# Negated row maxima of an attention kernel: one identity product and a DMA in place of eight transposes and two row copies

## What is computed

```python
scores = jnp.einsum('bhqd,bhkd->bhqk', q, k) * scale
scores = jnp.where(ki > qi, -jnp.inf, scores)
attn = jax.nn.softmax(scores.astype(jnp.float32), axis=-1).astype(q.dtype)
out = jnp.einsum('bhqk,bhkd->bhqd', attn, v)
```

## Time and profile before

| | us |
|---|---|
| median of 3 runs | 1096.61 |
| lowest and highest | 1094.93, 1104.24 |
| the profiled execution | 1103.35 |
| its span in the profile | 1101.6 |

### The profile page before, as it was taken

One profiled execution on the slowest core, in us unless ns is written; L12 is line 12 of the kernel. 1 busy time (PEld: TensorE's weight loads), 2 busy tenths in 40 slices (PEclk: granted clock), 3 DMA queues, 4 the chain that ended last, 5 costly groups with the idle time before them and its releaser, 6 DMA issues.

```text
span 1101.6 us, 16371 instructions
## 1 busy us (share of the span) xinstructions
PE 1026.8 (93%) x5792; PEld 795.2 (72%) x5792; DVE 661.8 (60%) x1195; ACT 420.3 (38%) x669; POOL 635.3 (58%) x363
## 2 busy tenths in 40 slices
PE   3889999997999999986979999999999999999996
PEld 2666777774877777653768888878888788887885
DVE  6666887885787887852755445624446344553454
ACT  3215665563136565543132222333224222242222
POOL 4105878899227788887445445465544654546452
PEclk9989999998999999977979999999999999999998
DMA  6322332333212233211232232433233423233331
GB/s 217 96 51 77 84 85 69 91 90 97 93 48 75 75 81 84 73 39 58 97 133 86 91 109 87 134 114 115 86 115 105 143 86 114 87 115 134 114 105 39
DMA packets 52509, 104.38 MB, mean 95 GB/s; under 512 B 10848, under 2 KB 10848, under 8 KB 52192
## 3 DMA queue, kind: packets, MB, share of 16 engines
q1 hardware_dynamic: 52448, 103.59, 30.4%
HBM read 70.00 MB, written 8.39 MB: 71 GB/s over the span
## 4 chain that ended last, share of the span: by engine, by line
PE 76%; POOL 8%; DVE 7%; issue 5%; ACT 2%; SPq 1%; DMA 1%; POOLq 0%; ACTq 0%; DVEq 0%
PE ps L1159 18%; PE ps L1160 18%; PE ps L1161 18%; PE ps L1243 7%; PE ps L1215 6%; PE ps L1277 5%; POOL gu_lo L616 2%; POOL p_sum L600 2%; PE ps L1291 1%; PE ps L1226 1%; POOL acc L662 1%; PE ps L1251 1%; DMA x_in<-x 1%; DVE xt_lo L927 1%; POOL dn_lo L622 1%
## 5 line engine op out<-in xcount | busy, mean ns | idle before, releaser
L616 POOL TENSOR_TENSOR gu_lo<-gu_raw,gu_hi 128x1024 fp32r<-128x1024 f32 x64 | 155.2, 2425 | 234.4 <-ACT gu_hi L821 234.4
L950 DVE CUSTOM_DVE_ANT_0 ps<-ps,mask_q 128x384 f32<-128x384 f32 (+7 forms) x256 | 190.2, 778 | 38.1 <-PE ps L1215 35.2
L1159 PE MATMUL ps<-xt_hi,gu_hi 128*128 128x512 f32 x512 | 202.2, 395 | 7.6 <-POOL gu_lo L616 7.6
L1025 DVE TENSOR_TENSOR h<-ps,silu 128x512 f32<-128x512 f32 x64 | 44.2, 690 | 266.7 <-PE ps L1161 239.5
L1160 PE MATMUL ps<-xt_lo,gu_hi 128*128 128x512 f32 x512 | 201.3, 393 | 0.0
L1161 PE MATMUL ps<-xt_hi,gu_lo 128*128 128x512 f32 x512 | 201.0, 393 | 0.0
L1031 DVE TENSOR_TENSOR h_lo<-h,h_hi 128x512 fp32r<-128x512 f32 x64 | 154.2, 2409 | 2.2
L821 ACT ACTIVATE gu_hi<-gu_raw 128x1024 fp32r<-128x1024 f32 x64 | 67.9, 1061 | 147.7 <-PE ps L1161 110.1
L1243 PE MATMUL ps<-q_stack,k_stack 98*128 98x512 f32 (+3 forms) x384 | 116.0, 385 | 4.1 <-DVE q_stack L969 1.6
L1159 PEld LDWEIGHTS ps<-xt_hi,gu_hi 128*128 128x128 f32 x512 | 97.5, 190 | 29.4 <-issue 8.9
L1215 PE MATMUL ps<-k_stack,q_stack 96*128 96x512 f32 (+3 forms) x384 | 111.4, 366 | 5.2 <-DVE m_full L950 2.7
(11 more groups left out here) (124 smaller groups left out, 1817.7 us busy)
## 6 DMA issues: line engine op xcount, KB each, us to landing
gu_raw<-gu_w SPq DMA_DIRECT2D x64, 512.0 KB, 3.8
dn_raw<-dn_w SPq DMA_DIRECT2D x64, 256.0 KB, 2.6
x_in<-x SPq DMA_DIRECT2D x32, 256.0 KB, 4.1
q_stack<-st_hi SPq DMA_DIRECT2D x128, 64.0 KB, 2.0
k_stack<-st_hi SPq DMA_DIRECT2D x128, 64.0 KB, 2.0
qk_raw<-qk_w SPq DMA_DIRECT2D x16, 256.0 KB, 3.0
q_stack<-st_lo SPq DMA_DIRECT2D x64, 64.0 KB, 2.0
k_stack<-st_lo SPq DMA_DIRECT2D x64, 64.0 KB, 2.0
```

The lines of the kernel that those rows point to most:

```text
L616: nc.gpsimd.tensor_tensor(gu_lo[:, s], gu_raw[:, s], gu_hi[:, s].bitcast(F32), ALU.subtract).then_inc(gu_split, 1)
L950: nc.vector.tensor_tensor_reduce(out=scores, in0=scores, in1=mask_q[:, SEQ - (t + 1) * P:], scale=1.0, scalar=MASKED, op0=ALU.add, op1=ALU ...
L1159: nc.tensor.matmul(dst, hi, r_hi, start=start, stop=False)
```

## The change

The maxima now go to rows by one product and one DMA. DVE writes the 32 columns (hi for head 0 and 1, eight tiles each, then the rests in the same order) into a small tile `m_cols`. The PE multiplies `m_cols`, as the stationary operand, by an identity of type float32r: the result has 32 partitions, one for each (part, head, tile), and 128 columns, one for each query of the tile. DVE copies these 32x128 values to `m_rows` (a corner of `x_in[:, 4]`), and ACT's queue issues one DMA that lays them out as two rows of 2048 in `q_stack`. `scores(g, 0)` waits for the DMA (`m_loaded`). DVE frees the two ring banks once its copy is done. On the PE the product stands behind three slices of the projection and ahead of the late values. Slice 3 now stands ahead of the scores of round 0. POOL makes `ident_r` once at the start.

```diff
-        m_spread = x_in[:, 4, 0:TT * M_STEP].rearrange("p (t n) -> p t n", n=M_STEP)
+        m_rows = x_in[0:2 * 2 * TT, 4, P:2 * P]
...
+            nc.gpsimd.tensor_copy(ident_r[:, :], ident[:, :]).then_inc(pool_hi, 1)
...
@@ scalar
-            def max_rows(g):
-
-                use = use_of_rows(g)
-                act.wait_ge(bank_full, use + NCH)
-                first = use % RING * CH
-                nc.scalar.activation(q_stack[QK_ROWS:ROWS, g % 2, 0], ps_cols[0:2, first:first + SEQ], ACT.Copy).then_inc(m_rows0, 1)
+            def load_maxima(g):
+
+                act.wait_ge(m_copied, g + 1)
+                to = q_stack[QK_ROWS:ROWS, g % 2].rearrange("p h (t n) -> p (h t) n", n=P)
+                act.dma_start(to.bitcast(F32), m_rows).then_inc(m_loaded, DMA)
 
             def body(g):
                 projected = g + 2 < ALL_UNITS
+                load_maxima(g)
                 if g % UNITS:
                     copy_acc(g - 1)
-                max_rows(g)
@@ vector
-                negative = ps[:, use % RING, 0:2 * TT].rearrange("p (t h) -> p t h", h=2)
-                m_hi, m_lo = m_spread[:, :, 0:HD + 1:HD].bitcast(F32R), m_spread[:, :, 1:HD + 2:HD].bitcast(F32R)
+                negative = ps[:, use % RING, 0:2 * TT].rearrange("p (h t) -> p h t", h=2)
+                m_hi, m_lo = (m_cols[:, n * 2 * TT:(n + 1) * 2 * TT].rearrange("p (h t) -> p h t", h=2) for n in range(2))
...
             def max_rows(g):
 
                 use = use_of_rows(g)
                 vec.wait_ge(bank_full, use + NCH)
-                first = use % RING * CH
-                nc.vector.tensor_copy(q_stack[QK_ROWS:ROWS, g % 2, 1], ps_cols[HD:HD + 2, first:first + SEQ]).then_inc(bank_free, NCH)
+                if g:
+                    vec.wait_ge(m_loaded, DMA * g)
+                nc.vector.tensor_copy(m_rows, ps[0:2 * 2 * TT, use % RING, 0:P]).then_inc(m_copied, 1)
+                vec.wait_ge(m_copied, g + 1)
+                vec.sem_inc(bank_free, NCH)
@@ tensor
-                for t in range(TT):
-                    at_col = use % RING * CH + t * P
-                    last = nc.tensor.transpose(ps_cols[:, at_col:at_col + P], x_in[:, 4, t * M_STEP:t * M_STEP + P], ident[:, :])
-                last.then_inc(bank_full, NCH)
+                nc.tensor.matmul(ps[0:2 * 2 * TT, use % RING, 0:P], m_cols[:, :], ident_r[:, :], start=True, stop=True).then_inc(bank_full, NCH)
...
                 if r == 0:
-                    pe.wait_ge(m_rows0, g + 1)
-                    pe.wait_ge(bank_free, use_of_rows(g) + NCH)
+                    pe.wait_ge(m_loaded, DMA * (g + 1))
...
-                project_next(0, 0)
+                project_next(0, 0, 1, 2)
+                transpose_maxima(g)
                 if has_sums(g):
                     values(g - 1, LATE_VALUES)
-                transpose_maxima(g)
-                project_next(0, 1)
                 maxima_of_next(0)
-                project_next(0, 2)
-                maxima_of_next(1)
-                pe.wait_ge(m_rows0, g + 1)
-                maxima_of_next(2)
+                project_next(0, 3)
+                maxima_of_next(1, 2)
                 scores(g, 0)
-                maxima_of_next(3)
-                project_next(0, 3)
-                maxima_of_next(4, 5)
+                maxima_of_next(3, 4, 5)
                 scores(g, 1)
```

More of the change, by code:

```diff
@@ L88 @@
 assert sorted(m[:2] for m in MAXES) == [(h, t) for h in range(2) for t in range(TT)]
-M_STEP = 48
 MAX_OFF = [sum(m[2] for m in MAXES[:n]) for n in range(len(MAXES))]
@@ L274, in build @@
             ident = sb(att, "ident", [P, P])
+            ident_r = sb(att, "ident_r", [P, P], F32R)
+            m_cols = sb(att, "m_cols", [P, 2 * 2 * TT], F32R)
             ident_bf = sb(att, "ident_bf", [P, P], BF16)
@@ L337, in build @@
         m_ready = sem("m_ready")
-        m_rows0 = sem("m_rows0")
+        m_copied = sem("m_copied")
+        m_loaded = sem("m_loaded")
         score_full = sem("score_full")
@@ L561, in _ @@
             pool.wait_ge(pool_hi, 8)
+            nc.gpsimd.tensor_copy(ident_r[:, :], ident[:, :]).then_inc(pool_hi, 1)
+            pool.wait_ge(pool_hi, 9)
             nc.gpsimd.tensor_copy(ident_bf[:, :], ident[:, :]).then_inc(consts_made, 1)
@@ L565, in _ @@
             pool.wait_ge(consts_made, 2)
-            made = [8]
+            made = [9]
             def split(hi, lo, raw, done):
@@ L956, in negated @@
                 vec.wait_ge(bank_free, use)
-                negative = ps[:, use % RING, 0:2 * TT].rearrange("p (t h) -> p t h", h=2)
-                m_hi, m_lo = m_spread[:, :, 0:HD + 1:HD].bitcast(F32R), m_spread[:, :, 1:HD + 2:HD].bitcast(F32R)
-                nc.vector.tensor_scalar(negative.bitcast(F32R), m_full[:, :, :], -1.0, None, ALU.mult).then_inc(dve_unit, 1)
+                negative = ps[:, use % RING, 0:2 * TT].rearrange("p (h t) -> p h t", h=2)
+                m_hi, m_lo = (m_cols[:, n * 2 * TT:(n + 1) * 2 * TT].rearrange("p (h t) -> p h t", h=2) for n in range(2))
+                m = m_full.rearrange("p t h -> p h t")
+                nc.vector.tensor_scalar(negative.bitcast(F32R), m, -1.0, None, ALU.mult).then_inc(dve_unit, 1)
                 vec.wait_ge(dve_unit, g + 1)
                 nc.vector.tensor_copy(m_hi, negative).then_inc(m_ready, 1)
-                nc.vector.scalar_tensor_tensor(m_lo, m_full[:, :, :], -1.0, negative, ALU.mult, ALU.subtract).then_inc(m_ready, 1)
+                nc.vector.scalar_tensor_tensor(m_lo, m, -1.0, negative, ALU.mult, ALU.subtract).then_inc(m_ready, 1)
             def max_rows(g):
```

## The result

| | before | changed |
|---|---|---|
| median, us (20 runs each) | 1100.59 | 1096.87 |
| lowest and highest | 1094.93, 1106.28 | 1092.17, 1102.12 |
| the profiled execution; its span | 1103.35; 1101.6 | 1096.35; 1094.5 |

The forecast was 1.0 us. The measured 1096.87 us lies inside the forecast's own range, 1092 to 1098, with the help of luck: the forecast of 1095.6 stands on a median of three runs, 1096.61, and the median of twenty is 1100.59. Taken from there, 1.0 us less is 1099.6, and that misses the measured time by 2.7 us.

A forecast was written before the change was run, and what follows sets the result against it. PE work fills the ordinary unit, but POOL's additions leave 0.39 us of slack; ten units give -3.4 us, uncovered units +2.4, so -1.0 us and 1095.6 us from a median of 1096.61. Range 1089 to 1104, the forecast's own 1092 to 1098.

The forecast's parts named there:

- A unit gains its slack, 0.4 us, not 0.7: Ordinary unit: `total` can come only 0.4 us earlier before POOL holds it, though PE work shrinks by 0.69 us.
- the sum: All units: ten ordinary units -3.4 us, uncovered units 0, 8 and 15 +1.6, +0.3 and +0.5, together -1.0 us.
- From the scores to `total` there were 2.66 us, now 1.97: Ordinary unit on the PE: this stretch shortens because the fourth slice moved ahead, putting `total` at B + 7.5.
- B: The instant when a unit's `body` begins on the PE with the projection slice, 150.28 us in the unit read.
- The ring: Scores of round 4, exponentials, 15.2 us of POOL, `total`, 4.9 us of PE to next round 4: closes in 22.0 us.
- the sign, a gap of 0.15: Ordinary units: `total` begins 0.15 us after POOL's last addition, with PE idle time put down to POOL.
- The rival of the whole saving: Twelve ordinary units gain the whole PE saving, 0.69 us each: 1090.7 us, chance 0.17.
- The row path: From product at B + 2.17 through DVE's copy and the DMA to the scores: 3.33 us, landing taken as 2.5.
- The cover of the transfer: PE work ahead of the scores ends at B + 5.5, just covering the transfer; gone once landing exceeds 2.9 us.
- the late transfer as a rival: The row transfer lands late and bounds every unit's scores: 1102.2 us at 3.3 us landing, 1105 at 3.5; chance 0.24.
- The ten units: Units 0 to 4 gain 1.69 us and units 8 to 12 gain 1.73 us, -3.4 us together.
- the clock as a rival: Unit 0: the PE stands about 1.9 us before the first scores, the clock falls, costing 1.5 us: 1097.1 us, chance 0.06.

The follow-up runs named there:

- run 7: Changed kernel with one maxima step moved behind the scores of round 0: 1096.74 us, ratio 0.9969 to the kernel before.
- run 8: Changed kernel with the projection's last slice put back between the scores of rounds 0 and 1: 1103.71 us, ratio 1.002 to the kernel before.
- run 3: Changed kernel (one product, one DVE copy, one DMA) with the PE's order of before: 1105.67 us, ratio 1.0035 to the kernel before.
- run 2: Kernel before with the PE's new order and ACT's row copy ahead of its accumulator copy, transposes and row copies kept: 1106.8 us, ratio 1.0067.

## Why the prediction was right, and where not

*Size and sign.* "A unit gains its slack, 0.4 us, not 0.7" came out as 0.33, and units 0 to 13 gave -1.3 us against the -1.5 that the sum has for them (-3.4, +1.6 and +0.3; its last +0.5 is for unit 15). The measured -3.7 us has a second part that the sum didn't hold, so the sign was right for a reason and the absolute time by luck, as said with the result.

*The step that failed* is "From the scores to `total` there were 2.66 us, now 1.97". It measured 2.29. With the scores at B + 5.66 and not at B + 5.5, the PE was ready for `total` at B + 7.95 and not at B + 7.5. Moving a slice out from between two rounds doesn't only shorten the path, it takes away the cover of ACT's exponentials. The head of the body adds up like this: transposes 0.85 to product 0.15, -0.70; slices -0.05; the first maxima, which now follow the values directly, +0.10; waits for ACT +0.30; together -0.35, against -0.32 by the two values of `total` less B.

On that +0.10: where the values (products with 32 columns of weights, `128*32`) and full ones meet, the distance grows by 0.1 us, from 0.18 to 0.28 for the first maxima and from 0.68 to 0.79 for a slice ahead of the values. The Trainium skill (TensorEngine Tiling (Array Packing), Key Properties) says that a change of the tiling mode drains the TensorE; these rows agree. The price isn't the same everywhere: in unit 0 the new product, `128*32` too, stands between full ones, starts 0.23 us behind the slice as any other would, and adds only 0.05 to the step after it (84.43 to 84.66, 0.23 instead of 0.18).

*The bound by POOL.* The ring was worked out as 22.0 us, and runs 7 and 8 both stop at 22.01 with `total` 0.14 and 0.16 us after POOL. As a limit it was right. As what holds the changed kernel it was wrong: the PE with its new wait holds it at 22.07. The two limits lie so close that the sum hit the unit by luck. The prediction named the sign, a gap of 0.15; it measured 0.18 to 0.24 in most units, and I first read that as "held".

*The rival of the whole saving* fell for two reasons at once: the wait on ACT, and POOL at 22.0 behind it.

*The row path.* Product at B + 2.17 forecast, B + 2.20 measured. DVE's copy 0.30, measured 0.28. Product to scores 3.33 forecast, 2.81 to 2.99 measured where the scores waited, but for body 15 of run 3. Two terms were over-sized: product to DVE's copy, 0.42 forecast and 0.26 measured, and issue to scores, 2.22 to 2.40 us against the 2.56 taken (2.50 and 0.06). So unit 0's scores came 1.43 us later, not 1.81, and `total` of unit 0 0.89, not 1.6; from the product or first transpose to the scores, unit 8 took 2.81 us against 2.96 before and unit 15 took 2.84 against 2.67, so the one lost nothing and the other 0.2, where 0.3 and 0.5 were charged. The cover of the transfer holds, 3.46 us of work against 2.9, and the late transfer as a rival fell. Run 3 shows what it would have been: 0.5 us of idle time and 0.67 us of distance per unit. What the rival named as its reason, SP's loads on the same engines, did show once, in body 15 of run 3.

The transfer carries 32 rows and makes 34 packets, two more than rows. The Trainium skill (DMA: Bandwidth & Descriptors, section on why a DMA increments its semaphore by 16) gives two engines for this shape and one semaphore write for each engine; the two extra packets agree with that. In the changed kernel the transfer wasn't slow: the rule leaned towards a rival that fell.

*The ten units.* 1.69 us for the first batch, measured 1.59. 1.73 for the second, measured 1.05, since unit 10 gained only 0.09 (22.31 us) and the last of that row nothing. Unit 6 lost 0.33, as expected, where POOL runs without a pause.

*The clock.* At the same clock the table gives 2.2 us, so of the 3.7 us some 1.5 go with it. Of the 2.2, units 0 to 13 have 1.3; where the other 0.9 lie, these profiles don't tell. The prediction had the clock as a rival of one sign, in unit 0; unit 0 ran at 1.00. The last two units, which were charged with +0.5 us, are where it moved in the two profiles compared. Two profiles of the changed kernel show 0.92 to 0.93 there and the single one of the kernel before 0.81 and 0.73. Whether the change brings this or only meets it, no run here isolates.

## What to carry to other kernels

Before you move work out of a place on the busiest engine, list what that work covered there: here a slice between two rounds hid the exponentials that free the banks, and its move cost 0.3 of the 0.7 us saved. An in-order engine's place in the plan is shared: a step moved on the PE needs the matching move on ACT, or it can cost far more than it brings (12 to 14 us here). When a unit has two limits within 0.1 us of each other, as here, a gap in the timeline doesn't tell which one holds; relieving one of them in both kernels did. A short transfer is only as early as what stands ahead of it on the DMA engines: look at the other queues' loads at its place in every body, not in an ordinary one alone.

## What the runs showed of the hardware

A matmul that waits 0.15 us for its bank shows no idle time, since the modelled end of the one before covers it; only the starts betray it, set beside the end of ACT's row. In the changed kernel and in runs 2 and 7 such a start lies 0.05 to 0.06 us behind that end.

The time of this kernel goes with its mean granted clock, 6 to 7 us less per 0.01, more than the whole change is worth, and kernels with the same ordinary unit differ in it: 0.963 and 0.970 in runs 8 and 7, both at 22.01 us.

A transfer of 16 KB in 32 rows, SBUF to SBUF on ACT's queue, let the waiting scores start 2.22 to 2.40 us after its issue, and 4.7 us after it where 1 MB of loads had been issued 0.46 us ahead of it.

Adding one partition-wise reduction of 128 columns for two heads to `total` cost the PE 0.2 us, and saved POOL 0.73.
